# A fused attention and expert kernel: score banks tiled by 64 queries with two heads stacked, ten banks a batch instead of twelve

## The reference, cut to what matters

```
x = x + layernorm(attention(layernorm(x)))      # 16 heads of 8, causal
x = x + layernorm(experts(layernorm(x)))        # 8 experts, each token takes the one with the highest affinity
attention: scores = Q K^T / sqrt(8), -inf above the diagonal, softmax over keys, times V, times WO
experts:   tokens sorted by expert; y = xs + relu(layernorm(xs) w1 + b1) w2 + b2; out = a*y + (1-a)*xs
```

## Time and profile before

| what | us |
|---|---|
| median of 3 runs (lowest to highest) | 454.77 (454.33 to 455.31) |
| the profiled execution | 454.81 |
| its span, first to last instruction | 453.1 |
| TensorE busy | 359.6, 79% |
| VectorE busy | 336.5, 74% |
| ScalarE busy | 250.8, 55% |
| GpSimd busy | 242.1, 53% |

### The profile page before, as it was taken

One profiled execution on the slowest core, in us unless ns is written; L12 is line 12 of the kernel. 1 busy time (PEld: TensorE's weight loads), 2 busy tenths in 40 slices (PEclk: granted clock), 3 DMA queues, 4 the chain that ended last, 5 costly groups with the idle time before them and its releaser, 6 DMA issues.

```text
span 453.1 us, 11940 instructions
## 1 busy us (share of the span) xinstructions
PE 359.6 (79%) x3739; PEld 286.3 (63%) x3739; DVE 336.5 (74%) x1244; ACT 250.8 (55%) x574; POOL 242.1 (53%) x334
## 2 busy tenths in 40 slices
PE   3359688979989998999899898987525798999960
PEld 1136466656767777777677766765424688888860
DVE  7748776758877887887887889575551788989880
ACT  2204457556675675675675665574203577777750
POOL 3803254534474664664664664567360266767773
PEclk9999989989999999999999999899555999999995
DMA  7661853726535535535526527021024466666720
GB/s 207 109 104 41 135 90 48 112 57 94 90 66 78 91 71 72 98 64 79 99 51 93 95 42 117 26 63 34 14 85 128 116 165 170 174 172 176 186 58 9
DMA packets 34686, 42.83 MB, mean 95 GB/s; under 512 B 5465, under 2 KB 25053, under 8 KB 33088
## 3 DMA queue, kind: packets, MB, share of 16 engines
q1 hardware_dynamic: 31744, 37.43, 42.3%
q0 software_dynamic: 2304, 4.37, 2.9%
q10 hardware_dynamic: 576, 0.27, 0.2%
HBM read 30.59 MB, written 11.66 MB: 93 GB/s over the span
## 4 chain that ended last, share of the span: by engine, by line
PE 54%; DMA 11%; DVE 9%; issue 9%; POOL 6%; SPq 5%; ACT 4%; POOLq 0%; DVEq 0%; ACTq 0%
PE O L846 6%; DMA aug<-nmT 6%; PE O L1006 5%; PE ST L825 5%; PE S L812 4%; PE S L993 4%; PE M L858 3%; PE M L772 3%; PE S L807 3%; PE S L805 3%; PE S L802 3%; PE O L850 3%; PE ST L993 2%; PE ST L834 2%; POOL out_x L516 2%
## 5 line engine op out<-in xcount | busy, mean ns | idle before, releaser
L1082 DVE TENSOR_REDUCE nmf<-S 128x2 f32<-128x512 f32 (+1 forms) x192 | 130.1, 680 | 53.7 <-PE S L812 26.7
L421 POOL TENSOR_SCALAR_AFFINE_SELECT p<-p 128x512 f32<-128x512 f32 x64 | 40.8, 638 | 96.9 <-ACT p L583 96.9
L583 ACT ACTIVATE p<-ST 128x1024 f32<-128x1024 f32 x64 | 65.5, 1023 | 16.6 <-PE ST L825 15.9
L812 PE MATMUL S<-aug 126*128 126x128 bf16 x512 | 51.7, 225 | 0.0
L825 PE MATMUL ST<-aug 128*128 128x256 bf16 x256 | 39.9, 279 | 14.9 <-DMA aug<-nmT 14.7
L425 POOL TENSOR_SCALAR_AFFINE_SELECT p<-p 128x512 f32<-128x512 f32 x64 | 40.9, 639 | 10.4 <-ACT p L587 7.8
L516 POOL DMA_INDIRECT out_x<-vaug,x_all x39 | 40.7, 1045 | 8.3 <-issue 6.1
L812 PEld LDWEIGHTS S<-aug 126*128 126x128 bf16 x512 | 41.2, 101 | 3.8
L526 POOL TENSOR_TENSOR rsz<-vez,mhalf 128x1 f32<-128x1 f32 x39 | 22.1, 567 | 39.0 <-DVE vez L1437 38.9
L1006 PE MATMUL O<-w_tab,vaug 128*128 x312 | 42.6, 280 | 0.0
L846 PE MATMUL O<-p,vaug 128*32 128x256 f32 x512 | 41.2, 391 | 0.3 <-POOL p L421 0.3
(11 more groups left out here) (155 smaller groups left out, 868.4 us busy)
## 6 DMA issues: line engine op xcount, KB each, us to landing
w1s<-in_w1x SPq DMA_DIRECT2D x39, 259.0 KB
qk_parts<-qkp SPq DMA_DIRECT2D x16, 384.0 KB, 2.8
aug<-qk_parts SPq DMA_DIRECT2D x32, 192.0 KB
aug<-qk_parts SPq DMA_DIRECT2D x32, 128.0 KB
x_all<-xs_rows SPq DMA_DIRECT2D x39, 67.0 KB, 2.4
aug<-qk_parts SPq DMA_DIRECT2D x32, 64.0 KB
w_tab<-in_w2t SPq DMA_DIRECT2D x8, 256.0 KB, 5.6
out_x<-vaug,x_all POOLq DMA_INDIRECT x39
```

What stands on the lines that cost most here:

```text
L421: g.affine_select(out=v, in_=v, compare_op=ALU.is_ge, fill=0.0, base=0, pattern=[[0, 4], [1, P]], channel_multiplier=-1).then_inc(s["sel0" ...
L583: a.activation(p0[:, gr % 2], ST0[:, :, :], ACT.Exp, scale=SCALE).then_inc(s["exp0"], 1)
L812: last = mm(bank[:, j * SEQ + kb * P:j * SEQ + (kb + 1) * P], q[:, h, P:SEQ], k[:, h, kb * P:(kb + 1) * P], start=False, stop=(j == 1 and ...
L1082: v.tensor_reduce(dst, S[:, n % 2].rearrange("p (j n) -> p j n", j=k), op=ALU.max, axis=AX_X, negate=True).then_inc(s["red"], 1)
```

## The change

The first pass uses 64 queries as weights instead of 128. Two heads h = 0 and 1 stand in rows 0 to 63 and 64 to 127 of a bank. With quarters 0 to 3 of 64 queries, quarter j needs 64 (j + 1) keys. Each half of 8 heads takes five banks: kinds 0 and 1 hold quarter 3 (256 keys) of four heads each, kind 2 holds quarter 1 (128 keys) of all eight heads, kinds 3 and 4 hold quarters 2 (192 keys) and 0 (64 keys) of four heads each. The mask covers only the diagonal blocks of 64 columns and is added last, by a matmul that is 128 wide. Even groups have three banks and odd groups two. The banks of kinds 3 and 4 are reduced by two instructions (192 and 64 columns). The shift goes out by two DMAs per half instead of one. `hot`, `run` and their constants become bf16, so the rank matmuls (L905, L906) are bf16; a constant is taken off and added again so that the numbers stay exact. On VectorE `alphas` moves from early in the step to around the second `divide`, and `shift_parts` of half 0 comes before instead of after the bank of group 2, u = 0. VectorE builds the mask from a 128 by 128 triangle before it clears `qaug`.

```diff
             def shift(b, half):
...
-                sp.dma_start(qaug[SHIFT:P, p, 8 * half:8 * half + 8].rearrange("c h (q t) -> c (h q) t", t=P),
-                             nmT[:, p, half]).then_inc(sh_in[half], 16)
+                for h in (0, 1):
+                    at = 8 * half + 4 * h
+                    sp.dma_start(qaug[SHIFT:P, p, at:at + 4].rearrange("c h (j t) -> c (h j) t", t=QB),
+                                 nmT[:, p, half, QB * h:QB * h + QB]).then_inc(sh_in[half], 16)
...
+        def unit(gr, u):
+
+            return 5 * (gr // 2) + 3 * (gr % 2) + u
+
+        def units(gr):
+
+            return 2 if gr % 2 else 3
...
-                if u == 0:
-                    mm(bank, identb[:, :], causal[:, :, :], start=True, stop=False)
-                    for j in range(4):
-                        h = 4 * gr + j
-                        last = mm(bank[:, j * P:(j + 1) * P], q[:, h, 0:P], k[:, h, 0:P], start=False, stop=(j == 3))
...
-                    mm(bank.rearrange("p (j c n) -> p j c n", j=2, c=2)[:, :, 1], identb[:, :], causal[:, 0:2],
-                       start=True, stop=False)
+                def score(pair, quarter, col):
+
+                    keys = QB * (quarter + 1)
+                    for h in (0, 1):
+                        head = 8 * half + 4 * h + pair
+                        mm(bank[QB * h:QB * h + QB, col:col + keys], q[:, head, QB * quarter:QB * quarter + QB],
+                           k[:, head, 0:keys], start=(col == 0), stop=False)
+
+                if kind < 2:
+                    for r in (0, 1):
+                        score(2 * kind + r, 3, 2 * P * r)
+                    masked, blocks = bank.rearrange("p (r n) -> p r n", r=2)[:, :, 3 * QB:4 * QB], 2
+                elif kind == 2:
+                    for r in range(4):
+                        score(r, 1, P * r)
+                    masked, blocks = bank.rearrange("p (r n) -> p r n", r=4)[:, :, QB:P], 4
                 else:
+                    for r in (0, 1):
+                        score(2 * (kind - 3) + r, 2, 2 * P * r)
+                        score(2 * (kind - 3) + r, 0, 2 * P * r + 3 * QB)
+                    masked, blocks = bank.rearrange("p (r n) -> p r n", r=2)[:, :, 2 * QB:4 * QB], 4
+                mm(masked, identb[:, :], causal[:, 0:blocks], start=False, stop=True).then_inc(s["s_r"], 1)
...
-                    mm(rank_m, before[:, :], last.pick(hot, 2, 2), start=True, stop=False)
-                    ins = mm(rank_m, ones[:, :], last.pick(run, 2, 2), start=False, stop=True)
+                    mm(rank_m, beforeb[:, :], last.pick(hot, 2, 2), start=True, stop=False)
+                    ins = mm(rank_m, onesb[:, :], last.pick(run, 2, 2), start=False, stop=True)
...
             def maxima(b, gr, u):
...
+                    if kind < 2:
+                        last = most(3, 2 * kind, 2, two)
+                    else:
+                        most(2, 2 * (kind - 3), 2, two[:, :, 0:3 * QB])
+                        last = most(0, 2 * (kind - 3), 2, two[:, :, 3 * QB:4 * QB])
...
+            dve.wait_ge(s["consts"], 5)
+            for low_q in (0, QB):
+                v.tensor_copy(causal[low_q:low_q + QB], triangle[low_q:low_q + QB, low_q:low_q + QB].unsqueeze(1)
+                              .to_broadcast([QB, 4, QB])).then_inc(s["mask_d"], 1)
             v.memset(qaug[:, 1].bitcast(F32), 0.0).then_inc(s["qzero"], 1)
```

More of the change, by code:

```diff
@@ L154, in sandwich_kernel @@
         key = sb("key", [P, NT])
-        hot = sb("hot", [P, NT, E])
-        run = sb("run", [P, NT + 1, E])
+        hot = sb("hot", [P, NT, E], BF16)
+        run = sb("run", [P, NT + 1, E], BF16)
+        run0 = sb("run0", [P, E])
         rank = sb("rank", [P, NT, E])
@@ L473, in _ @@
             g.iota(fill_at[:, :], [[0, 1]], base=E * CAP, channel_multiplier=1).then_inc(s["ids_r"], 1)
-            for table, by, base in ((down, -1, E), (steps, P, 0), (slots, 1, 0), (starts, CAP, 0), (run[:, 0], CAP // P, 0)):
+            for table, by, base in ((down, -1, E), (steps, P, 0), (slots, 1, 0), (starts, CAP, -BASE), (run0, CAP // P, -P)):
                 g.iota(table[:, :], [[by, table.shape[-1]]], base=base, channel_multiplier=0,
                        allow_small_or_imprecise_dtypes=True).then_inc(s["consts"], 1)
+            pool.wait_ge(s["consts"], 11)
+            for table, by in ((run[:, 0], run0), (beforeb, before), (onesb, ones)):
+                g.tensor_copy(table[:, :], by[:, :]).then_inc(s["consts"], 1)
             pool.wait_ge(s["ids_r"], 3)
@@ L563, in shift_out @@
                 if b.follows(RING):
-                    act.wait_ge(sh_in[half], b.times(16, 16 * (1 - RING)))
+                    act.wait_ge(sh_in[half], b.times(32, 32 * (1 - RING)))
                 p = b.slot(RING)
@@ L791, in scores_by_query @@
             def scores_by_query(b, gr, u):
-                p = b.slot(RING)
-                n = 3 * gr + u
+                if u >= units(gr):
+                    return
+                p, n = b.slot(RING), unit(gr, u)
+                half, kind = n // 5, n % 5
                 if n == 0:
@@ L797, in scores_by_query @@
                 if b.k > 0 or n >= 2:
-                    pe.wait_ge(s["red"], b.times(12, n - 1))
+                    pe.wait_ge(s["red"], b.times(UNITS, n - 1))
                 bank = S[:, n % 2]
                 q, k = qaug[0:SHIFT, p], kaug[0:SHIFT, p]
-                if u == 0:
-                    mm(bank, identb[:, :], causal[:, :, :], start=True, stop=False)
-                    for j in range(4):
-                        h = 4 * gr + j
-                        last = mm(bank[:, j * P:(j + 1) * P], q[:, h, 0:P], k[:, h, 0:P], start=False, stop=(j == 3))
-                else:
-                    mm(bank.rearrange("p (j c n) -> p j c n", j=2, c=2)[:, :, 1], identb[:, :], causal[:, 0:2],
-                       start=True, stop=False)
-                    for j in range(2):
-                        h = 4 * gr + 2 * (u - 1) + j
-                        for kb in (0, 1):
-                            last = mm(bank[:, j * SEQ + kb * P:j * SEQ + (kb + 1) * P], q[:, h, P:SEQ],
-                                      k[:, h, kb * P:(kb + 1) * P], start=False, stop=(j == 1 and kb == 1))
@@ L973, in _ @@
             take_m()
-            mm(M[:, 0:E], ones[:, :], run[:, NT], start=True, stop=True).then_inc(s["total_r"], 1)
+            mm(M[:, 0:E], onesb[:, :], run[:, NT], start=True, stop=True).then_inc(s["total_r"], 1)
             pe.wait_ge(s["rt"], 1)
@@ L1073, in maxima, with most @@
             def maxima(b, gr, u):
-                p = b.slot(RING)
-                n = 3 * gr + u
-                dve.wait_ge(s["s_r"], b.times(12, n + 1))
-                if u == 0:
-                    dst, k = nmf[:, p, 4 * gr:4 * gr + 4, 0], 4
-                else:
-                    dst, k = nmf[:, p, 4 * gr + 2 * (u - 1):4 * gr + 2 * u, 1], 2
-                v.tensor_reduce(dst, S[:, n % 2].rearrange("p (j n) -> p j n", j=k), op=ALU.max, axis=AX_X,
-                                negate=True).then_inc(s["red"], 1)
+                if u >= units(gr):
+                    return
+                p, n = b.slot(RING), unit(gr, u)
+                half, kind = n // 5, n % 5
+                dve.wait_ge(s["s_r"], b.times(UNITS, n + 1))
+                def most(quarter, first, count, src):
+                    return v.tensor_reduce(nmf[:, p, half, first:first + count, quarter], src, op=ALU.max, axis=AX_X,
+                                           negate=True)
+                if kind == 2:
+                    last = most(1, 0, 4, S[:, n % 2].rearrange("p (r n) -> p r n", r=4))
+                else:
+                    two = S[:, n % 2].rearrange("p (r n) -> p r n", r=2)
+                    if kind < 2:
[3 more added lines that the diff above has]
+                        last = most(0, 2 * (kind - 3), 2, two[:, :, 3 * QB:4 * QB])
+                last.then_inc(s["red"], 1)
             def maxima_and_stats(i, b, gr, u):
                 maxima(b, gr, u)
-                if i.k < 2:
-                    x_stats(i.k + 3, 3 * gr + u)
+                if i.k < 2 and u < units(gr):
+                    x_stats(i.k + 3, unit(gr, u))
             def shift_parts(b, half):
                 p = b.slot(RING)
-                src = nmf[:, p, 8 * half:8 * half + 8].rearrange("p h q -> p (h q)")
-                dve.wait_ge(s["red"], b.times(12, 6 * half + 6))
+                src = nmf[:, p, half].rearrange("p r j -> p (r j)")
+                dve.wait_ge(s["red"], b.times(UNITS, 5 * half + 5))
                 if b.follows(RING):
@@ L1267, in _ @@
             for gr in range(NG):
-                for u in range(3):
+                for u in range(units(gr)):
                     maxima(Nth(0), gr, u)
@@ L1302, in step @@
                     ln_variance(l2, 0)
+                if l4:
+                    alphas(l4, 0)
                 if old:
                     divide(old, 1)
```

(2 more changed lines are left out.)

35 lines of the change are left out of this document (19 added, 16 removed).

## The result

The median went from 454.55 us (452.79 to 455.31, four runs) to 463.9 us (462.59 to 469.92, four runs), a ratio of 1.018 (1.0135 to 1.022). Slower was right, and the time lies in the range; the predicted 461 is 3 us short. The profiled execution took 463.67 us for 454.81 before. Its page, parts 1, 4 and 5, shows in part 1 why no share of busy time would have told the sign: TensorE, its weight loads and VectorE are all less busy than in the earlier trace rows, in a longer run.

A forecast was written before the change was run, and what follows sets the result against it. TensorE's work (part B) and an engine chain (part A) pace nine late steps, DMAs five early ones: 9 x (0.68 - 0.27) = 3.7 plus 5 x 0.65 = 3.3, +7.0 on 454.8: 461.8, said 461; range 450 to 470.

The forecast's parts named there:

- The banks, part B: Step from L787 to next L772, TensorE's own work: new banks 0.485 or 0.54 us, +1.05; +0.68 with the ranks.
- part A: Step from first L772 to the shift's transposition L787, a chain over engines, 4.69 us: shorter by 0.27.
- Rival (1): Weight loads bound the 64-wide banks, or two tiles do not run at once: +12, 473 us; 1 in 10.
- Rival (3): Switching between 64 and 128 wide on TensorE costs next to nothing: 447 to 453 us; 12 in 100.
- rival (4): VectorE, not TensorE, paces the step, and each step saves 0.8 us of reductions: 444 us; 8 in 100.
- Rival (2): No change: TensorE's extra goes into part B's stalls, the second DMA into SyncE's slack: 454.8 us; 13 in 100.
- The ranks: L905 and L906 in part B: in bf16 at most 0.11 us together, perhaps 0.08; -0.37 us a step.
- The shift's second DMA: On SyncE ahead of `parts_out`, moving it 0.65 us: DMA loop about 17.1 us, +0.65 in each of five early steps.
- Still covered where B sets the step: The DMA loop of about 17.1 us stays hidden in steps set by TensorE's work in part B.
- 2.6 + 0.7 + 2.8 + 10.2 = 16.3 us: DMA loop of one step before the change, L825 to next L825: under the 17.24 us step by less than a microsecond.
- 1.3 if the landing comes late in the later steps too: Upper end for the shift's second DMA, where +0.65 us in each early step was taken.
- The early steps: First five attention steps, where DMA already sets the pace: 5 x 0.65 = 3.3 us slower.

The follow-up runs named there:

- a_out_between: The changed kernel with the parts' write issued between the two DMAs of the shift's half 1 instead of behind both: 459.66 us, 1.010 to before.
- a_fp32_ranks: The changed kernel with the rank matmuls in fp32 again: 468.79 us, 1.034 to before.
- experiment 5: Rank matmuls alone to bf16 in the kernel before: 451.77 us, step 17.01; and back to fp32 in the changed kernel: 468.79 us.
- experiment 6: The kernel before with `residue` on VectorE ahead of the reduction of the last bank: 455.28 us, 0.999 to before.
- b_two_cols: The kernel before with each half's shift sent by two DMAs, both rows and half of the columns each: 465.16 us, 1.020 to before.
- b_residue_first: The kernel of experiment 6, the kernel before with `residue` ahead of the last bank's reduction: 455.28 us, 0.999 to before.
- b_two_dmas: The kernel before with each half's shift sent by two DMAs, one for each of its two rows: 475.01 us, 1.042 to before.

## Why the prediction was right, and which of its steps were not

**The banks, part B: right.** Predicted 0.485 and 0.54 us a bank, found 0.50 and 0.56. In the steps of 17.68, part A (first L793 to L808) is 4.39 us (235.80 to 240.19), so B is 13.29: +0.74 for the +0.68 predicted. The step is longer by 0.44, predicted 0.41; nine of them 4.0 us, predicted 3.7. That this counts in the time is shown by a_out_between (steps of 17.68 and little else) and by the ranks, whose 0.39 us appears in the step of a_fp32_ranks. Rival (1), loads that bound, would have taken 0.45 us for the 64-wide part; it took at most 0.35 with the switch. Rival (3), a free switch, fell with the 0.093 us, and rival (4), VectorE as the one that paces, with the steps of after: two reductions fewer didn't shorten them. Something of it was true: where experiment 5 shortened the step, 0.16 us came back as a wait for a reduction; the 0.14 of experiment 6 may be the same, but no view names it. Rival (2), no change, fell with the median.

**The ranks and part A: right.** -0.39 a step for -0.37 predicted; A 4.39 for 4.69, -0.30 for -0.27. L785's stall grew by 0.34 us a step (0.34 to 0.68), what the disappeared bank had covered, and `alphas` cost nothing.

**The shift's second DMA: the step that failed.** Its size in the queue was right, 0.66 us (L307 1.37 behind the shift instead of 0.71). "Still covered where B sets the step" was wrong, for two reasons. The loop was mis-sized: 2.6 + 0.7 + 2.8 + 10.2 = 16.3 us has its last term from one step in which the shift landed early (187.35 to 197.55). The step before has 10.75 (170.13 to 180.88), and the loop by those rows is 2.2 + 0.6 + 0.7 + 2.8 + 10.75 = 17.05; after, 17.8. And the room was taken as fixed, though the change takes 0.5 us of it in part A: L857 may come 2.12 us behind the first L793, L825 might 2.65. So nine late steps lost 5.2 us beside TensorE's 4.0, and 5.4 came back in a_out_between: 3.1 by the 0.66 of the queue, the rest with the length of three writes and with the last step. The bound "1.3 if the landing comes late in the later steps too" named the case but not how it comes about.

**The early steps: wrong too, the other way.** +3.3 was predicted, -0.65 came. The traces account for nearly all of this 3.9. The third of the five (20.26 us before, 17.82 after) is the case that the prediction named: `parts_out` waits for GpSimd's `low` (80.23, issue 80.25), so the queue's 0.65 is hidden. In it and in the fifth `parts_out` took 3.74 and 3.55 us before, after it 2.8, which gives back 1.7. And in the third TensorE ran at half its clock behind the shift in before, and at the full clock in after:

```profile
93.29 1.04 PE L825 MATMUL ST<-aug 128*128 128x256 bf16 x4 [3.06 <-DMA aug<-nmT]
```

```profile
93.34 0.61 PE L857 MATMUL ST<-aug 128*128 128x256 bf16 x4 [1.97 <-DMA aug<-nmT]
```

The granted clock from 93.3 to 96.4 us is 0.50 before and 1.00 after; from these rows to the transposition it is 3.59 us (to 96.88) before and 2.27 (to 95.60) after, another 1.3. This is no accident of one run: in each of the seven other traces with the old tiling such a drop begins between 93.5 and 95.8 us, in none of the five with the new one. The prediction had no term for it. b_two_cols, which has the second DMA and also this drop, has +1.5 in these steps.

**Open.** The fourteen traces have 196 of these writes from 40 us on. All 16 that took over 4.2 us have a fetch of instructions beside them, but most writes with a fetch are not long: it goes by when it begins. Of 14 fetches that began 1.0 to 2.4 us behind the issue of the write 13 stand beside a long one, of 24 that began 2.4 to 2.8 us behind three, and the 34 that began from 0.5 us ahead to 0.8 behind left it at 2.76 to 3.74 us. No experiment removed or moved a fetch by itself: this is an association. So part of after's loss, 1.8 us by the count above, may be a matter of where the fetches fall. What the two short stalls of b_residue_first wait for isn't named by a view.

## What to carry to other kernels

Lay out each loop that closes around a step (an engine's work, a chain, the DMAs) from several steps, take the longest value of a term that ends in a wait, and ask what room the change's own gains take from the others: a loop that is "covered by less than a microsecond" is a second bound. What a split adds to an issuing queue is paid by all that stands behind it, so look first at what can go between the pieces; one moved call gave back over 4 of the 9 us that this change lost. A narrower tile pays about 0.1 us each way around it, and from 64 to 32 wide as well: it has to save more than 0.2 us in each place where it stands between full-width work.

## What the runs showed of the hardware that I had not expected

- Matmuls 64 wide in the two column tiles start 3 to 4 ns apart and run at the same time; the way in and the way out cost 0.09 to 0.10 us each, as for 32 wide.
- Two bf16 matmuls of 16 columns with their full weight loads take 0.05 us together; the same in fp32 took 0.45.
- A write of 384 KB took 2.76 us where nothing disturbed it, and 4.3 to 4.9 us in 13 of the 14 cases in which a 16 KB packet of instructions was fetched beside it 1.0 to 2.4 us behind its issue; fetches at other moments mostly left it under 3.8.
- A small DMA from ScalarE's queue moved no packet for 8 us while SyncE's queue was full (48.20 to 56.2 us), so a queue of its own didn't put it ahead.
- Behind the reads the packets of two DMAs into one row each went out over 3.0 to 5.7 us (b_two_dmas); those of one DMA with the same bytes into both rows over 0.4 to 1.25 (the kernel before), and of two such DMAs with half the columns each over 0.6 to 1.5 (b_two_cols).
- With the granted clock at 0.50 the same four matmuls took 1.04 us instead of 0.61, and the stretch behind them 3.59 instead of 2.27 (93.3 to 96.9 us): a wait for a DMA of 2 to 4 us was followed by this in some steps and not in others.
